# A routed feed-forward layer inside a two-layer gated transformer: tokens sorted by expert group, and half of the shared gate and up moved ahead

## The reference, cut to what matters

```python
x = _rmsnorm(src + sa, norm1_w)                 # src + self attention, per token
flat = x.reshape(S, C)                          # 800 tokens x 256
shared = _swiglu(flat @ W_shared_in) @ W_shared_out
g_probs = softmax(flat @ Wg_gate + group_bias)  # 2 groups of 4 experts
g_idx = argmax(g_probs, axis=-1)
e_logits = flat @ We_gate + expert_bias         # 8 experts
e_probs = softmax(where(in_group, e_logits, -inf))
p_expert = e_probs * g_prob
topv, topi = top_k(p_expert, 2)                 # both in the token's group
w = zeros((S, E)).at[arange(S)[:, None], topi].set(topv)
h = _swiglu(flat @ W1_shared)                   # the same for all experts
for e in range(8):
    routed = routed + h @ W2_experts[e] * w[:, e:e + 1]
out = _rmsnorm(x + shared + routed, norm2_w)
```

## Time and profile before

| | us |
|---|---|
| median of 3 runs | 583.16 |
| lowest, highest | 581.89, 585.56 |
| the profiled execution, its own time | 584.23 |
| its span, first to last instruction | 582.4 |
| PE busy | 532.8 (91%) |
| DVE busy | 282.0 (48%) |
| ACT busy | 183.7 (32%) |
| POOL busy | 125.6 (22%) |
| granted clock of PE, mean over the span | 0.976 |

### The profile page before, as it was taken

The page is one execution under the profiler, slowest core; times in us unless marked ns, Lnnn a source line. Parts: engine busy times, 40 slices in busy tenths (PEclk is TensorE's granted clock), DMA queues, the critical chain, the costliest instruction groups (busy, mean ns, idle before and its releaser), DMA issues. The chain is left out here.

```text
span 582.4 us, 9223 instructions
## 1 busy us (share of the span) xinstructions
PE 532.8 (91%) x3429; PEld 345.9 (59%) x3429; DVE 282.0 (48%) x660; ACT 183.7 (32%) x438; POOL 125.6 (22%) x146
## 2 busy tenths in 40 slices
PE   0989899899999879999999899999889999999995
PEld 0736575355556567788877677878535544544442
DVE  3436553121235575665676968887625222224242
ACT  1134331211103344555555545656532110000000
POOL 3112005001117252232232635341000000000000
PEclk9999968999999988999999999999989999999998
DMA  7989942279976697595573056000012000000000
GB/s 211 237 227 322 392 181 58 74 273 378 400 250 202 165 257 186 138 236 166 134 183 81 2 190 246 2 2 1 1 52 62 1 1 0 1 0 29 0 19 9
DMA packets 47087, 78.15 MB, mean 134 GB/s; under 512 B 6867, under 2 KB 36543, under 8 KB 46941
## 3 DMA queue, kind: packets, MB, share of 16 engines
q1 hardware_dynamic: 43841, 68.32, 38.0%
q0 software_dynamic: 3200, 9.22, 4.9%
HBM read 63.97 MB, written 12.13 MB: 131 GB/s over the span
## 5 line engine op out<-in xcount | busy, mean ns | idle before, releaser
L1392 PE MATMUL pb<-ring,big 128*128 128x512 f32 (+2 forms) x320 | 108.7, 593 | 2.3 <-DVE big L1343 1.2
L1392 PE MATMUL pb<-split 128*100 128x362 f32 (+2 forms) x320 | 78.3, 329 | 6.7 <-DVE nmx L1184 2.7
L1392 PEld LDWEIGHTS pb<-ring,big 128*128 128x128 f32 (+2 forms) x320 | 44.1, 166 | 59.4 <-issue 54.9
L1184 DVE TENSOR_REDUCE nmx<-pb 100x1 f32<-100x361 f32 x128 | 62.7, 527 | 25.6 <-PE pb L1392 25.2
L1392 PEld LDWEIGHTS pb<-split 128*100 128x100 f32 (+2 forms) x320 | 55.9, 183 | 16.7 <-issue 6.1
L860 ACT ACTIVATE big<-pb 121x400 f32<-121x400 f32 (+1 forms) x96 | 48.2, 505 | 23.9 <-PE pb L1392 21.6
L1364 DVE SCALAR_TENSOR_TENSOR ctxbuf<-pb,ctxbuf 128x256 f32<-128x256 f32 x48 | 23.2, 484 | 55.5 <-PE pb L1392 54.6
L1392 PE MATMUL pb<-big,arena 121*32 121x100 f32 (+3 forms) x1072 | 47.9, 264 | 1.5 <-ACT arena L710 1.2
L1392 PE MATMUL pb<-hT,ring 128*128 128x400 f32 x128 | 43.8, 501 | 0.5 <-DVE big L1343 0.5
L637 POOL TENSOR_TENSOR shift<-consts,nmx 100x400 fp32r<-100x400 f32 x32 | 28.3, 884 | 64.6 <-DVE nmx L1184 64.5
L1392 PE MATMUL pb<-hT,wgu 128*128 128x400 f32 (+2 forms) x108 | 39.7, 516 | 0.9 <-ACT hT L919 0.6
(11 more groups left out here) (242 smaller groups left out, 784.7 us busy)
## 6 DMA issues: line engine op xcount, KB each, us to landing
ring<-in_L_ffn_gate_up_proj SPq DMA_DIRECT2D x12, 1024.0 KB, 9.6
split<-kx_dram SPq DMA_DIRECT2D x64, 181.0 KB, 3.8
ring<-in_L_ffn_down_proj SPq DMA_DIRECT2D x12, 512.0 KB, 7.3
kx_dram<-split POOLq DMA_DIRECT2D x16, 362.0 KB, 4.9
ctxbuf<-in_L_ffn_gate_up_proj SPq DMA_DIRECT2D x4, 1024.0 KB, 9.6
ring<-in_L_ffn_W_experts SPq DMA_DIRECT2D x4, 1024.0 KB, 11.4
split<-qx_dram SPq DMA_DIRECT2D x64, 50.0 KB, 2.0
ctxbuf<-in_ctxT SPq DMA_DIRECT2D x6, 361.0 KB
```

The costliest lines, as they stand in the source:

```text
L1184: nc.vector.tensor_reduce(nmx[:, t % 4, q:q + 1], PB[SB[n % 3]][0:T, 0:CTX], AX.X, ALU.max, negate=True) \
L1392: return nc.tensor.matmul(o, l, r, start=start, stop=stop)
```

## The change: what it does

Tokens are sorted by group. Each token gets a slot: those of group 0 from slot 0 upward in their order, those of group 1 from slot 927 downward. The 928 slots (NS) make 8 tiles of ET = 116; each tile needs only 4 experts, and the offset of these in `w2n` is read into PE's registers (`value_load`), 8 times. A tile in which both groups would meet cannot arise, since 800 tokens leave 128 slots free.

The rows go by way of three new DRAM buffers: `es_dram` (normed rows, token number and logits, 267 wide), `ex_dram` (x) and `eb_dram` (normed row plus shared part), each written by 8 scatters of 100 rows from POOL and read back by SP in tiles of 116. All three are zeroed by 24 stores of 116 rows, which SP issues ahead of the eight weights in the middle of the cross attention. The output goes out by 8 scatters on POOL.

The shared part is computed before the sort, on batches: gate and up of the first half (units 0 to 3) stand between the closing steps of the self attention, those of the second half (4 to 7) after the logits, and its down projection (8 batches, 4 matmuls of 256 columns) after them. W1's 8 units run on sorted tokens, 464 columns instead of 400. Down then is 8 tiles of 2 banks, each 4 matmuls of 512 columns. The rows of the first four batches are normed during the last quads of the self attention (n = 28 to 30 on DVE). The weights `we` are computed from the sorted logits, after the rows are back.

The diff, cut to its core:

```diff
+ET = 116
+NS = NX * ET
+EX = D + 1 + 2 + NX
+FPARTS = [(0, 3), (3, 6), (6, 7), (7, 8)]
...
 # SP, in the cross attention
                 if b == 3:
                     sp.wait_ge(s("filled"), FILL["values"])
+                    for i in range(NX):
+                        sp.dma_start(es_dram[ET * i:ET * i + ET, :], zero_rows[0:ET, :]).then_inc(s("b_zero"), 16)
+                        for d in (ex_dram, eb_dram):
+                            sp.dma_start(d[ET * i:ET * i + ET, :], zero_rows[0:ET, 0:D]).then_inc(s("b_zero"), 16)
                     sp.dma_start(wq2, A["L1_ffn_Wq"].rearrange("(k p) n -> p k n", p=128)).then_inc(s("ld_wd"), 16)
...
+            sp.wait_ge(s("b_scat"), 2 * 16 * NB)
+            for g in range(NX // 2):
+                sp.dma_start(sorted_rows[0:ET, 2 * g:2 * g + 2, :],
+                             es_dram[2 * ET * g:2 * ET * (g + 1), :].rearrange("(i p) d -> p i d", p=ET)).then_inc(s(f"b_xg{g}"), 16)
+            sp.wait_ge(s("e_xst"), 16 * NB)
+            sp.dma_start(xF[0:ET], ex_dram.rearrange("(i p) d -> p i d", p=ET)).then_inc(s("ld_F"), 16)
+            sp.wait_ge(s("e_bst"), 16 * NB)
+            sp.wait_ge(s("n_tp"), NB // 2 * (turn("e") + 1) + NX // 2)
+            sp.dma_start(hF[0:ET], eb_dram.rearrange("(i p) d -> p i d", p=ET)).then_inc(s("ld_F"), 16)
+            sp.wait_ge(s("stored"), 16 * NX)
...
 # POOL
+            pool.wait_ge(s("b_slot"), 2)
+            for b in range(NB):
+                nc.gpsimd.indirect_dma_start(es_dram, bass.IndirectOffsetOnAxis(slot[:, b:b + 1], 0), stage(b), None,
+                                             bounds_check=NS - 1, oob_is_err=False).then_inc(s("b_scat"), 16)
+            pool.wait_ge(s("c_res"), NB)
+            for b in range(NB):
+                nc.gpsimd.indirect_dma_start(ex_dram, bass.IndirectOffsetOnAxis(slot[:, b:b + 1], 0), x[:, b, :], None,
...
+            for b in range(NB):
+                pool.wait_ge(s("e_base"), b + 1)
+                nc.gpsimd.indirect_dma_start(eb_dram, bass.IndirectOffsetOnAxis(slot[:, b:b + 1], 0), hN[:, b, :], None,
...
+            for part, (a, z) in enumerate(FPARTS):
+                inverse_root("f", stdF, rstdF, only=part)
+                for i in range(a, z):
+                    pool.wait_ge(s("f_out"), i + 1)
+                    nc.gpsimd.indirect_dma_start(flat_out, bass.IndirectOffsetOnAxis(tok[0:ET, i:i + 1], 0), xF[0:ET, i, :], None,
...
 # ACT, after the last quad
+            d_turned_copy(NB - 2)
+            d_sums_copy(NB - 1)
+            e_turned(0)
+            e_turned(1)
+            square(NB - 3)
+            shared_silu(0)
+            d_turned_copy(NB - 1)
...
 # DVE, self attention
+                if n == 28:
+                    rms_variance(0)
+                if n in (29, 30):
+                    rms_rows(0, range(2 * (n - 29), 2 * (n - 28)))
...
+            link(nc.vector.tensor_tensor(nflag, glT[:, :, 0], glT[:, :, 1], ALU.is_ge))
+            nc.vector.tensor_reduce(nsum, nflag, AX.X, ALU.add).then_inc(s("b_oh"), 1)
...
+            link(nc.vector.tensor_tensor(nslot, PB[5][0:T, 0:NB], nleft, ALU.add))
+            nc.vector.tensor_copy(slot[:], nslot).then_inc(s("b_slot"), 1)
...
 # PE, after the last quad
+            ln_pe("e", range(0, 2), stage, E_TURN)
             d_to_tokens(NB - 1)
+            shared_unit(0)
             bank6_part("Y", NB - 2, 0)
             d_turn_back(NB - 1)
+            shared_unit(1)
             bank6_part("Y", NB - 1, 0)
+            shared_unit(2)
+            ln_pe("e", range(2, 3), stage, E_TURN)
+            shared_unit(3)
+            ln_pe("e", range(3, 4), stage, E_TURN)
...
+            shared_unit(4)
+            pe.wait_ge(s("b_oh"), 2)
+            mm(PB[5][0:T, 0:NB], consts[0:T, cs["lower"]], nflag, True, False)
+            for d in range(1, NB):
+                mm(PB[5][0:T, d:NB], ones[0:T, 0:T], nflag[:, 0:NB - d], False, d == NB - 1)
+            mm(PB[5][0:T, NB:NB + 1], ones[0:T, 0:T], nsum, True, True).then_inc(s("b_pos"), 1)
+            for u in range(5, 2 * FT):
+                shared_unit(u)
+            pe.wait_ge(s("b_slot"), 3)
+            for b in range(NB):
+                for f in range(FT):
+                    last = mm(PB[shared_bank(b)][0:T, 0:D], hidS[:, f, T * b:T * b + T], wdn[:, f, :], f == 0, f == FT - 1)
+            for g in range(NX // 2):
+                pe.wait_ge(s(f"b_xg{g}"), 32)
...
+                        last = nc.tensor.transpose(PB[4 + g % 2][:, at:at + ET], sorted_rows[0:ET, 2 * g + q, 128 * k:128 * k + 128],
...
+            for u in range(2 * FT, 4 * FT):
...
+                        last = mm(PB[W1_BANKS[u % 3][w]][:, 0:4 * ET], wgu2[:, 1, k, F * w + 128 * f:F * w + 128 * f + 128],
+                                  hTs[:, k, 4 * ET * half:4 * ET * (half + 1)], k == 0, k == KT - 1)
+            first = [pe.value_load(offs[0:1, i:i + 1], min_val=0, max_val=EPG * D) for i in range(NX)]
             pe.wait_ge(s("e_hid"), 4 * FT)
+            for i in range(NX):
+                for p in range(2):
...
+                        last = mm(PB[v % 8][0:ET, :], hidE[:, f, ET * i:ET * i + ET], w2n[:, f, bass.ds(first[i] + 2 * D * p, 2 * D)],
+                                  f == 0, f == FT - 1)
```

More of the change, by code:

```diff
@@ L335, in build @@
         LN_PARTS = dict(a=[(0, NB)], b=[(0, NB - 2), (NB - 2, NB)], c=[(0, NB // 2), (NB // 2, NB)], d=UNITS,
-                        e=[(0, NB - 2), (NB - 2, NB)], f=PARTS)
-        FILL = {n: i + 1 for i, n in enumerate(("ones", "pads", "rows", "values", "pads_again", "queries", "sums"))}
+                        e=[(0, NB // 2), (NB // 2, NB - 2), (NB - 2, NB)], f=FPARTS)
+        FILL = {n: i + 1 for i, n in enumerate(("ones", "pads", "rows", "values", "pads_again", "queries"))}
         def roots(st, part):
@@ L909, in _, with e_turned, shared_silu @@
                 d_probs_copy(m)
[L910 to L917, removed]
+            def e_turned(g):
                 act.wait_ge(s("n_tp"), NB // 2 * turn("e") + g + 1)
-                nc.scalar.activation(hT[:, :, 2 * T * g:2 * T * (g + 1)], bank3(g % 2, KT, 2 * T), ACT.Copy) \
+                nc.scalar.activation(hT[:, :, 2 * T * g:2 * T * (g + 1)], bank3(E_TURN[g], KT, 2 * T), ACT.Copy) \
                     .then_inc(s("n_hT"), 1)
[L921 to L932, removed]
+            def shared_silu(u):
                 act.wait_ge(s("e_gu"), u + 1)
@@ new lines, in _ @@
+            d_turned_copy(NB - 2)
[5 more added lines that the diff above has]
+            d_turned_copy(NB - 1)
+            square(NB - 2)
+            shared_silu(1)
+            square(NB - 1)
+            shared_silu(2)
+            e_turned(2)
+            shared_silu(3)
+            e_turned(3)
+            for u in range(4, 2 * FT):
+                shared_silu(u)
+            for g in range(NX // 2):
+                act.wait_ge(s("n_tp"), NB // 2 * (turn("e") + 1) + g + 1)
+                nc.scalar.activation(hTs[:, :, 2 * ET * g:2 * ET * (g + 1)], bank3(4 + g % 2, KT, 2 * ET), ACT.Copy) \
+                    .then_inc(s("n_hT"), 1)
@@ L1247, in _, with rms_variance, rms_rows @@
                 rotations(t)
+            def rms_variance(part):
+                a, z = LN_PARTS["e"][part]
+                dve.wait_ge(s("d_sq"), z)
+                nc.vector.tensor_scalar(std[:, a:z], rsum[:, a:z], 1.0 / D, RMS_EPS, ALU.mult, ALU.add).then_inc(s("n_var"), 1)
+            def rms_rows(part, batches=None):
+                dve.wait_ge(s("n_std"), roots("e", part))
+                for b in batches or range(*LN_PARTS["e"][part]):
+                    nc.vector.scalar_tensor_tensor(out=stage(b)[:, 0:D], in0=hN[:, b, :], scalar=rstd[:, b:b + 1],
+                                                   in1=brow["n1"][0:T], op0=ALU.mult, op1=ALU.mult).then_inc(s("n_hN"), 1)
             def d_residual(b):
@@ L1392, in mm, with ln_pe @@
                 return nc.tensor.matmul(o, l, r, start=start, stop=stop)
-            def ln_pe(st, groups=range(NB // 2)):
+            def ln_pe(st, groups=range(NB // 2), row=lambda b: hN[:, b, :], banks=(0, 1, 0, 1)):
                 for g in groups:
                     pe.wait_ge(s("n_hN"), NB * turn(st) + 2 * g + 2)
-                    if g >= 2:
+                    if g >= 2 and banks[g] < 2:
                         pe.wait_ge(s("n_hT"), NB // 2 * turn(st) + g - 1)
@@ L1824, in _, with shared_unit @@
                     d_turn_back(b - 2)
+            def shared_unit(u):
+                half, f = u // FT, u % FT
+                if u >= 2:
+                    pe.wait_ge(s("e_hid"), u - 1)
+                if u % FT == 0:
+                    pe.wait_ge(s("n_hT"), NB // 2 * turn("e") + 2 * (half + 1))
+                for w in range(2):
+                    for k in range(KT):
+                        last = mm(PB[S_BANKS[u % 2][w]][:, 0:HALF], wgu2[:, 0, k, F * w + 128 * f:F * w + 128 * f + 128],
```

(9 more changed lines are left out.)

287 lines of the change are left out of this document (140 added, 147 removed).

## The result

The changed kernel takes 593.78 us (median of 4 runs, 593.05 to 596.62), the kernel before 582.52 beside it (4 runs, 580.39 to 585.56): a ratio of 1.0198 [1.0141, 1.0256]. It is slower by 2.0%, with 1.4 to 2.6% as the interval. The profiled execution took 593.42 for a span of 591.4 us.

A forecast was written before the change was run, and what follows sets the result against it. It took PE, busy for 91% of the span, as the bound. A gain of 19.7 us for all but the zero stores and 25.1 lost to them gave +5.4, rounded to +5: 588 us on the median, range 575 to 600.

The forecast's parts named there:

- The forecast case: Whole kernel: 588 us on the median, with its own range of 579 to 595; chance 0.60.
- Zero stores: Cross attention: 24 stores on four DMA engines delay batch 4's queries; PE waits 23.7 us, then restarts slowly; +25.1 us.
- the rival at 65 GB/s: Cross attention: zero stores run at the 68-row piece's rate, taking 44 us; PE waits 33, total 597 us; chance 0.22.
- The hidden fill: Cross attention: zero stores use all engines, only SP's issuing counts; PE waits 1 to 8 us, total 567; chance 0.10.
- Closing steps to positions: Self attention's end through logits to position sums: PE's list sums to 27.3 us, including 1.2 for norming.
- The cover: Closing steps: moved shared units hide the waits between them; if not, at most 5.4 us of idle returns.
- Sorted rows: Before W1: four queued loads of 3.0 us each, the last landing at 471; PE waits some 4 us in all.
- W1: Experts' gate and up on sorted tokens: 464 columns make 64 instructions take 25.2 us instead of 21.7; loss 3.5.
- Register loads: Before down: eight loads into PE's registers cost 0 to 4 us, taken as 1.
- Down: Down projection on sorted tiles: 128 instructions at 0.43 take 55.0 us; with the shared part, gain 30.3.
- the third rival: Sort not hidden: closing-step waits of 5.4 us stay, register loads cost 4; net +13, 597 us; chance 0.08.
- The end: After PE's last matmul: 3.5 us to DVE's last product, then 3.9 for a scatter and 0.4; about 1.3 lost.

The follow-up runs named there:

- late fill: Changed kernel with its 24 zero stores of 116 rows moved behind the loads of the experts' weights; 566.53 us, ratio 0.9665 to the kernel before.
- pauses alone: Changed kernel, zero stores behind the expert weights' loads, sorted-row loads uncut, POOL pausing between scatters of sorted rows, x and base; 563.29 us, ratio 0.9693.

## Why the prediction was right, point by point

The forecast case held: 593.8 lies in its own range of 579 to 595, near the upper end, slower by more than 1%, and the deciding term is the one named. But the sum itself, 588, lay just inside 1%, and most of the 0.46 for "slower" came from two rivals that fell. That several terms of the sum agree so closely is in part luck, as the points show. Forecasts are given in the profile's times, with the 25.1 us of the fill put in:

- **Zero stores**, +25.1: right in mechanism and total, off in the parts. Kernel before with the stores alone: +25.6. PE waited 24.55 (forecast 23.7), and the share was 0.26 to 0.28 (0.25). The rate was 92 GB/s, not 83, so the rival at 65 GB/s fell, and the fill was through at about 278, not 284.5. From there to PE's first scores it took some 15 us, not 9. So the queries were there at 293.07 (293.5) by luck: some 6 us too much for the fill and 6 too little for what is queued behind it cancelled. The restart at half clock cost 2.5 us, not 1.4. The hidden fill fell too, though its bounds fit stores of 128 rows: PE waits 6.7 us there, within its 1 to 8. The shares of 0.27 for 116 rows and 0.98 for 128, times 16, come to about 4 and 16 engines. By the Trainium skill ("DMA: Bandwidth & Descriptors", section "Why a DMA increments its semaphore by 16 and not by 1") the number of engines is the largest up to 16 that divides the slowest dimension of both sides, which is 4 and 16: the traces agree at both sizes.
- **Closing steps to positions**: the quads ended at 441.2 (forecast, with 1.2 for the norming, 441.7). From there 26.1 were forecast and 22.2 measured, mainly since I took 4.0 for logits of 2.92 and 3.1 for sums of 1.8. The cover held: PE was busy for 21.9 of the 22.2 us. Units 5 to 7 and the shared down took 22.1 us against 23.2, so PE was 5.8 us ahead of the forecast when it came to the sorted rows.
- **Sorted rows**: SP's load came 13.6 us behind the position sums (13.8). The forecast had the last of the sorted rows land 14.4 us behind that load; the trial with pauses shows 15.4 (454.56 to 469.96), the last two 3.0 apart as forecast. The wait of PE is the step that failed: between the shared down and W1 I had 5.5 us, 4 of them idle, and there are 12.1, with 8.5 idle (window 485.5 to 497.5). That is over the 6 us which I had named as a sign of being wrong. What ended it was not the loads but the late ACT and DVE of the hold-up, which no row of before could price. Beyond the loads this costs some 5 us, 60.9 (late fill) against 56.3 (pauses alone) in the table.
- The last two points cancel, which is luck again: 5.8 us early and 6.6 us more of sort. W1 began at 497.4 (forecast 496.6), down at 524.8 (525.0).
- **W1** took 26.0 us (forecast 25.2 and 1 of wait). **Register loads** 0, not 1: the wait ahead of down is 1.41, the silu and the product. **Down** 55.2 (55.0), ended 580.0 (580.0). So the third rival fell: nothing of the closing steps' waits was left, and no register load was seen.
- **The end** is mis-sized: from down's last matmul 11.4 us, forecast 7.8. The last product ends at 583.5, the span at 591.4: 7.9, where 4.3 was forecast. I took the scatter of layer 0 up to SP's next load. At the end there are 1.0 us of "issue", 1.6 of POOL's queue, and some 5 more of transfer and closing. Not all of the 3.6 need be the last scatter's: in the kernel before with 24 more scatters, SP's store still came last, and the end was 2.0 us longer. What takes these 2.0 was not tested.

So the sum was 3.6 us short in the profile. Up to the end of down the errors had cancelled, and the 3.6 of the end stayed; the other 2 us from 588 to 593.8 are the two executions' places beside their medians (1.1 above 583.16, 0.4 below 593.78) and rounding. Against the 582.52 measured beside it the change costs 11.3 us, where I said 5.

## What to carry to other kernels

Count the rows of each transfer before placing it in a queue that the critical engine depends on: 24 stores of 116 rows cost 25 us where 128 rows cost 6 and a later place nothing. When a sum comes out right, check the terms at several points of time: here steps 5.8 us too long in sum hid one 6.6 us too short, and behind the latter lay the 11 us (in the traces) that pauses between scatters and split loads gave back. A price taken from the middle of a kernel leaves out what the end adds. A wait on the critical engine is priced with the slow restart behind it, here some 2.5 us.

## What was not expected of the hardware

- Transfers on few engines hold up the queue that issues them: SP needed 1.24 us a store in the fill, with the DMA share at 0.27.
- With 16 or 21 indirect scatters in a row and loads of scattered rows beside them, ACT and DVE took up work about 10 us late, PE's single matmuls ran 1.1 to 1.4 us apart at POOL's pace of 1.30 us a scatter, and all of it was released 2 to 3 us after POOL paused. This held in every kernel with such a run (in four of them pauses from 464.5, 463.0, 476.5 and 492.0, with release at 467.4, 465.8, 478.7 and 495.1; with the units not moved POOL slipped one scatter in between, and the release at 476.1 came 1.4 us behind it). It is seen in none with groups of eight, and it is absent with 24 scatters beside which SP issues no load after the second. How the signals are held is open.
- 128 matmul instructions whose columns are addressed by a register take 0.43 us each, like those with a fixed address.
